# One cross-attention stage of a fused four-layer kernel: the two matmul kinds of each step in one array tiling, single steps, and the next batch's tiles on a new raster

## The reference, cut to what matters

```python
def _L3_xattn_ref(x, context, Wq, Wk, Wv):      # x (4, 256, 256) normalised, context (4, 1601, 256)
    q = x @ Wq.T; k_raw = context @ Wk.T; v_raw = context @ Wv.T
    # 32 heads of width 8; k and v are the even and the odd columns of [k_raw, v_raw]
    q = _rmsnorm(q); k = _rmsnorm(k)            # over the 8 columns of a head
    scores = einsum('bhnd,bhmd->bhnm', q, k) * 8 ** -0.5
    out = einsum('bhnm,bhmd->bhnd', softmax(scores), v)
x = x + _L3_xattn_ref(_layernorm(x), ctx_2048, ...)
x = x + _L3_ffn_ref(_layernorm(x), ...)         # ternary weights, activations rounded to 8 bits
```

## Time and profile before

| | us |
|---|---|
| median of 3 runs | 2702.28 |
| the profiled execution, its own time | 2702.71 |
| its span (first to last instruction) | 2701.0 |
| PE, DVE, ACT, POOL busy over the span | 2480.9, 1725.4, 1487.4, 1360.3 |
| the 416 steps, first exponential to the end of the last | 2131.8 to 2643.1 |

### The profile page before, as it was taken

One profiled execution on the slowest core, in us unless ns is written; L12 is line 12 of the kernel. 1 busy time (PEld: TensorE's weight loads), 2 busy tenths in 40 slices (PEclk: granted clock), 3 DMA queues, 4 the chain that ended last, 5 costly groups with the idle time before them and its releaser, 6 DMA issues. The chain is left out here.

```text
span 2701.0 us, 42995 instructions
## 1 busy us (share of the span) xinstructions
PE 2480.9 (92%) x13668; PEld 1695.5 (63%) x13730; DVE 1725.4 (64%) x3340; ACT 1487.4 (55%) x3294; POOL 1360.3 (50%) x917
## 2 busy tenths in 40 slices
PE   6889999979999999999999999998698798989886
PEld 4567777746777777777777777777354333333333
DVE  3346667557877877887877787787214555555435
ACT  2235544445556566555566555564112577777895
POOL 0015655435666676666676666676102376767300
PEclk9889999999999999999999999999799799999999
DMA  4212232230001000010001000003202000000100
GB/s 154 81 53 82 88 94 72 70 122 7 10 17 45 17 17 17 1 45 17 17 17 44 2 17 17 17 1 126 100 12 61 17 15 17 15 17 15 48 1 16
DMA packets 42419, 108.03 MB, mean 40 GB/s; under 512 B 5044, under 2 KB 26040, under 8 KB 37048
## 3 DMA queue, kind: packets, MB, share of 16 engines
q1 hardware_dynamic: 40424, 102.41, 11.5%
q0 software_dynamic: 768, 2.10, 0.2%
q10 hardware_dynamic: 1008, 0.79, 0.1%
HBM read 99.91 MB, written 4.98 MB: 39 GB/s over the span
## 5 line engine op out<-in xcount | busy, mean ns | idle before, releaser
L1212 POOL TENSOR_TENSOR xn<-xn,l_p 128x512 f32<-128x512 f32 (+1 forms) x400 | 636.7, 1592 | 176.9 <-ACT l_p L1254 159.9
L2216 ACT ACTIVATE l_p<-psum 128x1024 f32<-128x1024 f32 x416 | 397.9, 1024 | 113.6 <-PE psum L2338 112.6
L1340 DVE TENSOR_TENSOR l_plo<-l_p,l_phi 128x512 fp32r<-128x512 f32 (+1 forms) x464 | 406.0, 876 | 63.5 <-ACT l_p L1254 41.6
L1253 ACT ACTIVATE l_phi<-psum 128x512 fp32r<-128x512 f32 (+1 forms) x464 | 279.3, 602 | 219.5 <-PE psum L447 139.8
L1389 DVE TENSOR_REDUCE l_mx<-psum 128x1 f32<-128x512 f32 (+2 forms) x512 | 306.2, 617 | 36.0 <-PE psum L1553 35.3
L2190 POOL TENSOR_TENSOR l_rs<-l_ms,half_power 128x32 f32<-128x32 f32 x45 | 245.0, 5463 | 111.5 <-DVE l_ms L2242 111.5
L1254 ACT ACTIVATE l_p<-psum 128x512 f32<-128x512 f32 (+1 forms) x464 | 280.9, 605 | 0.0
L1483 PE MATMUL psum<-l_m,l_ones 128*128 128x512 f32 (+1 forms) x464 | 232.8, 502 | 0.0
L2347 PE MATMUL psum<-l_p,l_vs 128*32 128x256 f32 x3328 | 226.4, 390 | 1.1 <-ACT l_p L2216 1.1
L1572 PE MATMUL psum<-l_w,l_ctx 128*128 128x256 f32 (+1 forms) x832 | 218.2, 385 | 8.5 <-ACT l_qa L1271 4.9
L1553 PE MATMUL psum<-l_kThi,l_qThi 128*128 128x512 f32 (+2 forms) x512 | 200.1, 428 | 5.0 <-DVE l_mx L1389 2.3
(11 more groups left out here) (378 smaller groups left out, 5140.0 us busy)
## 6 DMA issues: line engine op xcount, KB each, us to landing
w_stage<-in_L_w_dram SPq DMA_DIRECT2D x76, 384.0 KB, 3.0
l_w<-in_L_w_qkv_dram SPq DMA_DIRECT2D x16, 1024.0 KB, 4.9
l_ct<-in_ctx_tiles_dram SPq DMA_DIRECT2D x52, 128.0 KB
c_T<-in_ctx_T_dram SPq DMA_DIRECT2D x4, 1601.0 KB
l_ctx<-in_ctx_T_dram SPq DMA_DIRECT2D x4, 1601.0 KB, 6.8
c_N<-in_ctx_dram SPq DMA_DIRECT2D x4, 1536.0 KB
s_wg<-in_L_gate_dram SPq DMA_DIRECT2D x4, 1024.0 KB, 12.4
s_wu<-in_L_up_dram SPq DMA_DIRECT2D x4, 1024.0 KB, 14.5
```

The source lines that it names most:

```text
L1212: g_.tensor_tensor(l2_acc[k][0:r, :], first[0:r, :], l2_p[c % 3][0:r, :], ALU.add)\
L1253: act.activation(l2_phi[c % 3][0:r, :], src, ACT.Exp).then_inc(l2_e, 1)
L1340: v.tensor_tensor(l2_plo[c % 3][0:r, :], l2_p[c % 3][0:r, :], l2_phi[c % 3][0:r, :].bitcast(F32), ALU.subtract)\
L2216: act.activation(l3_p[ring(odd, c)][:, :], psum[:, (c % 2) * 2 * BANK:(c % 2 + 1) * 2 * BANK], ACT.Exp, scale=float(D3) ** -0.5).then_inc( ...
```

## The change

1. Values: each head's fp32 matmul becomes two, over rows 0 to 63 and 64 to 127 of the keys, into banks 4 and 5; 64 rows by 32 columns, eight places in the array. Groups alternate between two halves of those banks. DVE's `gather` adds the two banks (a copy and an addition out of PSUM, where one copy was).
2. Scores: each 64 by 128 matmul becomes four of 64 by 32, so they have the same tiling as the values.
3. PE goes by single steps: scores s+2, values s, then what is due.
4. The next batch's tiles stand on a raster of two per group of 13 steps, all written out, also on DVE and POOL. With j the step in the group: even tiles have their halves after j = 12 (of the group before) and 2, `squares` at 3, `power` at 4, `pairs` at 10, `turn` at 11; odd ones their halves after 5 and 8, `squares` at 9, `power` at 10, `pairs` at 4 and `turn` at 5 of the next group. The last tile (14) has its second half at 1, `squares` at 2, `pairs` at 9, `turn` at 10 of group 7.
5. `gather` stands at j = 0 of the next group, the transposes back (`output`) and `add_out` at j = 2. The values of a new group wait for the `gather` of the group before. `f3_early` stands behind `add_out`; the places of `f3_beside` move.

```diff
+        FIRST_HALF, SECOND_HALF = beside(-1, 5), beside(2, 8, 1)
+        SQUARES, POWER = beside(3, 9, 2), beside(4, 10, 3)
+        PAIRS, TURN = beside(10, MC + 4, 9), beside(11, MC + 5, 10)
...
-        def l3_batches(engine, pair, per=None, unrolled=False):
+        def l3_steps(step):
             for b in range(B):
-                new = b + 1 if b + 1 < B else None
...
+                for s in range(STEPS3):
+                    step(b, b + 1 if b + 1 < B else None, s)
...
+            def gather(b, n):
+                cols = n % 2 * S
+                v.wait_ge(l3_pv, b * STEPS3 + (n + 1) * MC)
+                dve_steps.then(v, v.tensor_copy(l3_o[n % 2][:, :], bank(4, S, cols)))
+                v.tensor_tensor(l3_o[n % 2][:, :], bank(5, S, cols), l3_o[n % 2][:, :], ALU.add).then_inc(l3_od, 1)
...
+            def step(b, new, s):                                     # DVE
+                n, j = s // MC, s % MC
+                done = (b, n - 1) if n else (b - 1, NG - 1)
+                if j == 0 and done[0] >= 0:
+                    gather(*done)
+                if j == OUT_AT and done[0] >= 0:
+                    add_out(*done)
...
+                if new is not None:
+                    if s in SQUARES:
+                        squares(new, SQUARES[s])
+                    if s in PAIRS:
+                        pairs(new, PAIRS[s])
+                    if s in TURN:
+                        turned(new, TURN[s])
...
-                for a in range(2):
-                    rows = slice(a * 2 * W3, (a + 1) * 2 * W3)
-                    queries = l3_qT[b % 2][rows, n, 2 * a:2 * a + 2, :].rearrange("p h s -> p (h s)")
-                    mm = pe.matmul(bank(c % 2 * 2 + a), l3_kT[b % 2][rows, n, j * P:(j + 1) * P], queries, start=True, stop=True)
+                for r in range(0, P, 32):
+                    for a in range(2):
+                        rows = slice(a * 2 * W3, (a + 1) * 2 * W3)
+                        queries = l3_qT[b % 2][rows, n, 2 * a:2 * a + 2, :].rearrange("p h s -> p (h s)")
+                        mm = pe.matmul(bank(s % 2 * 2 + a)[r:r + 32, :],
+                                       l3_kT[b % 2][rows, n, j * P + r:j * P + r + 32], queries, start=True, stop=True)
                 mm.then_inc(l3_s, 1)
...
+                    pe.wait_ge(l3_vsd, b * NG + n + 1)
+                    need(pe, l3_od, b * NG + n)
+                pe.wait_ge(l3_e, b * STEPS3 + s + 1)
                 for h in range(HG):
-                    mm = pe.matmul(bank(4 + a, S)[h * 32:(h + 1) * 32, :], l3_vs[a][:, j, h, :],
-                                   l3_p[ring(i, c)][:, h * S:(h + 1) * S], start=(j == 0), stop=(j == MC - 1))
+                    for a in range(2):
+                        rows = slice(a * P // 2, (a + 1) * P // 2)
+                        mm = pe.matmul(bank(4 + a, S, n % 2 * S)[h * 32:(h + 1) * 32, :], l3_vs[n % 2][rows, j, h, :],
+                                       l3_p[s % 4][rows, h * S:(h + 1) * S], start=(j == 0), stop=(j == MC - 1))
...
+            def step(b, new, s):                                     # PE
...
+                    scores(b, s + 2)
+                elif new is not None:
+                    scores(new, s + 2 - STEPS3)
+                values(b, s)
+                if j == OUT_AT and done[0] >= 0:
+                    output(*done)
+                if new is None:
+                    f3_beside(pe, n // 2, n % 2 * MC + j)
+                else:
+                    if s in TURN:
+                        turn(b, new, TURN[s])
+                    if s in FIRST_HALF:
+                        project(new, FIRST_HALF[s], 0)
+                    if s in SECOND_HALF:
+                        project(new, SECOND_HALF[s], 1)
```

More of the change, by code:

```diff
@@ L1916, in program, with beside @@
         PT = 4
-        BESIDE = [3, 7, 11, 15], [9, 14, 19, 24], [10, 15, 20, 25]
-        OUT_AT = MC + 3
-        assert PT * (NP - 1) == MC - 1 and N3 - PT * (NP - 1) <= PT
+        STEPS3 = NG * MC
+        N3X = N3
+        OUT_AT = 2
+        def beside(first, second, last=None):
+            at = {}
+            for q in range(N3X):
+                g = q // 2
+                if q == N3X - 1 and last is not None:
+                    at[(NG - 1) * MC + last] = q
+                elif q % 2 == 0:
+                    at[max(g * MC + first, 0)] = q
+                else:
+                    at[g * MC + second] = q
+            return at
+        FIRST_HALF, SECOND_HALF = beside(-1, 5), beside(2, 8, 1)
+        SQUARES, POWER = beside(3, 9, 2), beside(4, 10, 3)
+        PAIRS, TURN = beside(10, MC + 4, 9), beside(11, MC + 5, 10)
+        assert PT * (NP - 1) == MC - 1 and N3 - PT * (NP - 1) <= PT and N3 == 2 * NG - 1
         assert C3 % 2 == 0 and (2 * C3) % 4 == 0 and NP % 2 == 0
@@ L2180, in l3x_pool, with stage @@
             first_pool(g)
-            def stage(b, n, parity, before):
+            def stage(b, n, before):
                 need(g, l3_vsd, n + b * NG)
@@ L2185, in stage, with power @@
                 g.tensor_tensor(l3_none2[:, :], half_power[:, 0:1], half_power[:, 0:1], ALU.mult)
[L2186 to L2203, removed]
+                g.tensor_copy(l3_vs[n % 2][:, :, :, 0:D3], l3_v[b % 2][:, :, n * HG:(n + 1) * HG, :]).then_inc(l3_vsd, 1)
+            def power(new, q):
+                g.wait_ge(l3_msd, new * N3 + q + 1)
+                g.tensor_tensor(l3_rs[q % PT][:, :], l3_ms[q % PT][:, :], half_power[:, 0:H3], ALU.pow).then_inc(l3_rsd, 1)
+            def step(b, new, s):
+                n, j = s // MC, s % MC
+                if j == 0 and n + 1 < NG:
+                    stage(b, n + 1, b * STEPS3 + n * MC)
+                    if b == B - 1 and n == 0:
+                        f3_root(g, 0)
+                elif j == 0 and new is not None:
                     g.wait_ge(l3_kvd, 2 * (new * N3 + MC))
-                    stage(new, 0, 0, new * (NP * C3) - MC)
-            l3_batches(g, pair)
+                    stage(new, 0, b * STEPS3 + n * MC)
+                if new is not None and s in POWER:
+                    power(new, POWER[s])
+            l3_steps(step)
         def l3x_scalar(act):
@@ L2243, in squares, with pairs @@
                     .then_inc(l3_msd, 1)
-            def pairs(new, i, m, context):
-                v.wait_ge(l3_rsd, i * PT + (new * N3 + m + 1))
+            def pairs(new, q):
+                m = q % PT
+                v.wait_ge(l3_rsd, new * N3 + q + 1)
                 norm = heads(l3_n[:, :])
@@ L2277, in add_out @@
                                                   l3_rec[:, :, :].unsqueeze(3).to_broadcast([P, TB, HG, D3]), ALU.mult))
-                row = x[:, b * TB:(b + 1) * TB, bass.ds((i * 2 + a) * (HG * D3), HG * D3)]
+                row = x[:, b * TB:(b + 1) * TB, n * (HG * D3):(n + 1) * (HG * D3)]
                 v.tensor_tensor(row, row, l3_y[:, :, :, :].rearrange("p k h d -> p k (h d)"), ALU.add).then_inc(x_upd, 1)
[L2281 to L2297, removed]
@@ L2301, in l3x_tensor, with project @@
+            l3_steps(step)
+            gather(B - 1, NG - 1)
+            f3_early(v, NP - 1, 1)
+            add_out(B - 1, NG - 1)
         def l3x_tensor(pe):
             first_tensor(pe)
-            def project(new, i, m, context, half):
-                k = i * PT + (new * N3 + m)
+            def project(new, q, half):
+                k, m = new * N3 + q, q % PT
+                context = q < MC
                 if half == 0:
                     if context:
-                        loads = NP if m == 0 else NP - 1
-                        pe.wait_ge(l3_cland[m], i * 16 + (new * loads + 1) * 16)
+                        pe.wait_ge(l3_cland[m], 16 * (new * len(range(m, MC, PT)) + q // PT + 1))
@@ L2312, in project @@
                     need(pe, l3_kvd, k * 2)
-                lhs = l3_ct[m][:, half, :] if context else l3_xb[:, half, (m - 1) * P:m * P]
+                lhs = l3_ct[m][:, half, :] if context else l3_xb[:, half, (q - MC) * P:(q - MC + 1) * P]
                 mm = pe.matmul(bank(6, 2 * D if context else D), lhs, (l3_wkv if context else l3_wq)[:, half, :],
@@ L2349, in values, with output @@
                 mm.then_inc(l3_pv, 1)
[L2351 to L2356, removed]
+            def output(b, n):
+                pe.wait_ge(l3_od, b * NG + n + 1)
+                new = b + 1
+                if new < B:
+                    pe.wait_ge(l3_Td, new * N3 + min(2 * n + 1, N3))
@@ L2357, in out @@
                 else:
[L2358 removed]
+                    pe.wait_ge(x_upd, b * NG + n + X_AT[6])
                 for k in range(TB):
[L2360 removed]
+                    mm = pe.transpose(bank(7, P, k * P), l3_o[n % 2][:, k * P:(k + 1) * P], ident[:, :])
                 mm.then_inc(l3_oT, 1)
[L2363 to L2391 removed]
@@ L2393, in l3x_tensor, with step @@
-            scores(0, 0, 0)
-            scores(0, 0, 1)
-            l3_batches(pe, pair, unrolled=True)
-            out(B - 1, NP - 1, 1, None, True)
```

(13 more changed lines are left out.)

114 lines of the change are left out of this document (38 added, 76 removed).

## The result

| | before | after |
|---|---|---|
| median, runs of one chip (range) | 2702.45 (2701.83 to 2706.68, 4 runs) | 2727.74 (2720.80 to 2729.11, 4 runs) |
| ratio to before, 95% interval | | 1.0085 [1.0065, 1.0105] |
| profiled execution, its own time | 2702.71 | 2729.11 |
| first exponential of the stage | 2131.8 | 2136.2 |
| batches 0 to 2, from their first exponential to batch 3's | 405.3 | 431.4 |

The forecast was 2744, in a range of 2712 to 2786. The profiled executions differ by 26.4 us: 26.1 in the three batches with tiles to prepare, -5.1 in the last batch, 0.9 behind it, and 4.4 ahead of the stage, where nothing was changed. That last part belongs to the single execution: over the twelve profiles of this study the stage starts between 2130.2 and 2136.2, and a second profile of the same changed kernel has 2133.7.

The account below looks back on a forecast made before the run. It took PE as nearer the bound than ACT, except in the last batch, where ACT sets the pace. +33+13.5-5+0.8 = +42.3 on the profiled 2702.7 us, 0.4 over the median, gave 2744, range 2712 to 2786.

Parts of the forecast that it names:

- The rival with hidden stalls: At the turns: DVE's chain fits into the ring's time, a group takes 16.0 us, the kernel 2688; chance 12%.
- DVE's chain, half's end to turn: In the raster: from a half's end through `squares` and `pairs` to the turn, 3.73 us whatever PE does.
- Four steps held by the ring, 0.1 each: In each full group: the array starts empty and follows the sequencer after an exponential held it, 0.1 us per step.
- The ring's R: Between scores: if a step's scores come late, PE's step two further on starts no sooner than 1.60 us after them.
- The stall: At the turns: PE waits for `pairs` 1.42 or 1.43 us, some 43 times, near 60 us in all.
- sign of batches of 149 to 150 us: Among the signs that the forecast is right: batches of 149 to 150 us and a last one of 101.
- 15 groups: Groups 1 to 5 of three batches: 18.85 us each, before 16.65; +33 us in all.
- Batch changes: Groups 0, 6 and 7 around each batch change: 56.3 us, before 51.8; three times 4.5, +13.5 us.
- One tiling for a step: Scores and values on PE: with equal tiling the drains go, and a step takes 0.67 us.
- The last batch: Where ACT sets the pace: 12.4 us a group, 101 us in all, before 106.0; -5 us.
- The end: After the last exponentials: longer `gather` and a feed-forward step before the last `add_out`, +0.8 us.
- the sequencer as the bound: On PE: 33 ns an instruction would make a step 1.6 us and the kernel 2960 us; chance 2%.

Follow-up runs that it names:

- the first two experiments: Changed kernel with the even tiles' turn two steps later, 2697.9 us; then also the odd tiles' `pairs` two steps earlier, 2677.15 us.
- the second experiment: Changed kernel with the even tiles' turn two steps later and the odd tiles' `pairs` two steps earlier: 2677.15 us, ratio to before 0.9909.
- old-scores run: Changed kernel with only the scores put back to two matmuls of 64x128, values left at 64x32: 2759.55 us.

## Why the prediction was right, and where its size was off

The mechanism is the one forecast: PE stands still for DVE's `pairs` at the turns, ACT behind it, and the first two experiments take the stalls away one by one. The rival with hidden stalls has been built, in effect, by the second experiment, and so its condition is known: it isn't a smaller error of mine, it takes another order on DVE.

- **DVE's chain, half's end to turn.** Forecast 3.73 us, whatever PE does. In the rows above it is 3.50 (2339.97 to 2343.47). Two reserves I had added aren't there: `pairs` starts before the last of `squares` has ended (2341.81 against 2341.90), and the turn starts 0.06 after `pairs`, not 0.13. `pairs` itself takes 1.60, not 1.65. That is 0.23 twice a group, 0.46 of the 0.93 us by which the group came out below 18.85.
- **Four steps held by the ring, 0.1 each.** This term failed. I argued that when the sequencer had been held, the array follows its 48 instructions with a lag. Values start 0.23 after scores in such a step (2346.49 to 2346.72 in the timeline), and 0.22 in the others. The lag is 0.01 us, not 0.1.
- **The ring's R.** Forecast 1.60; measured 1.56 (2344.93 to 2346.49). ACT starts 0.48 after the scores do, 0.05 later than in the earlier trace rows, and the scores that it releases start some 0.05 after its end, where the earlier trace rows have 0.15. Three times 0.04 is 0.12 a group. With the other two: 0.46+0.4+0.12 = 0.98 for 0.93.

The quicker release isn't the tilings' doing. The stage's first released scores, in the new kernel with the old tilings and in the old kernel with the new ones:

```profile
2132.63 0.61 PE L2345 MATMUL psum<-l_qT,l_kT 64*128 64x512 f16 x2 [0.89 <-ACT l_p L2215]
...
2133.40 0.63 PE L2345 MATMUL psum<-l_qT,l_kT 64*32 64x512 f16 x8 [0.96 <-ACT l_p L2216]
```

The exponentials ahead of them end at 2132.57 and 2133.25. So 64x128 scores follow 0.06 later in the new kernel, and 64x32 scores 0.15 later in the old one. What differs is an edit that my list of the change left out: in the old kernel every step's scores wait for two semaphores (`l3_Td` and `l3_e`), and a wait instruction of its own (line 1139 in the earlier trace rows) stands ahead of the weight load; in the new one `l3_Td` is waited for at a batch's first step alone. No run makes that edit by itself.

- **The stall.** Forecast 1.42 and 1.43, some 43 times, near 60 us in all; measured 1.17 in the full groups, 45 times, 52.0. My comparison with 14.2 was with PEld's line, whose own successor is 73.6; PE's own goes from 3.9 to 52.0. My sign of batches of 149 to 150 us wasn't met: they take 143.7 to 144.1.
- **15 groups.** Forecast +33, measured 15*(17.92-16.66) = +18.9. This is the term that was mis-sized.
- **Batch changes.** Forecast 56.3 for the three groups, measured (431.4-15*17.92)/3 = 54.2, before 51.8: +7.2 instead of +13.5. Group 6 (17.1 for 18.2) and group 7 (20.4 for 21) carry the same reserves. (The three that I added up, 16.1, 18.2 and 21, make 55.3, not 55.4.)
- **One tiling for a step.** Forecast 0.67 us a step on PE, no drain, fp16 and fp32 alike; measured 0.65 to 0.66. The old-scores run shows that it is the equal tiling that does it.
- **The last batch.** Forecast 101 us, -5; measured 100.9, -5.1, of which 4.0 are there with the old tilings too. **The end**: forecast +0.8, measured +0.9.
- **Sum.** Forecast +42; measured, without the execution's own 4.4 ahead of the stage, 18.9+7.2-5.1+0.9 = +21.9 in the profiled execution, and +25.3 between the medians.

The rival of hidden stalls was also priced too high: 2688 with groups of 16.0; the runs have 2677 with 15.47. Of the others, the sequencer as the bound is out. The Trainium skill (TensorE: Matmul & The Clock Gate, Part 1) gives some 62 ns per matmul with hardware decoding off; by it, an estimate, 24 matmuls would hold a step at 1.49 us. The steps here follow one another in 0.65 to 0.66, so the trace doesn't agree. (With the rounding of the earlier trace rows the bound in my prediction was 28 ns a matmul, not 25.) The rule of the Trainium skill on tiling (TensorEngine Tiling (Array Packing), Key Properties), that a change of mode drains the array, agrees with the old-scores run, whose two modes differ in columns only: 0.32 us from scores to values and 0.59 back, where one tiling has 0.22 and 0.43.

So the change holds a gain and a loss: tilings worth 0.8 to 1.5 us in a full group, and other edits that cost some 2.1. 1.8 of these were lost because `squares` of one tile stood directly ahead of `pairs` of the other, with the turn one step behind. Two numbers turn +0.85% into -0.9%.

## What to carry to other kernels

When work is spread evenly over steps, count for each hand-over the whole chain on the slower in-order engine, with everything that stands ahead in its text, and place the consumer behind it; even spacing on PE says nothing about it. With a ring of two, a stall of PE is a stall of ACT, and no spare array time pays it back. A tiling of the array is a property of the whole step: in the new order one kind of matmul changed alone lost and both together won, and even both lost where the order was the old one. When a profile names no releaser for a wait, or one that looks right, compare the wait's end with the end of everything that the code waits for there.

## What the runs showed of the hardware

- Tilings that differ in columns alone cost time at each change: with 64x32 values and 64x128 scores a step took 0.91 us, against 0.65 to 0.66 with both at 64x32. The full groups were longer (18.90) than with both kinds at their old tilings (18.73, steps of 0.89).
- fp16 and fp32 matmuls of one tiling follow each other without a loss: 0.22 us after eight 64x512 fp16 streams start, the fp32 ones do.
- How soon scores start after the exponential that releases them didn't depend on their tiling: 0.05 to 0.06 us in the kernels whose scores wait for one semaphore (64x32 and 64x128), 0.15 in those whose scores wait for two (64x128 and 64x32).
- Steps of 48 PE instructions followed one another in 0.65 us, on average 14 ns each, and in a step that an exponential had held, values started 0.01 us later than in others.
